# Decoder layer with a routed feed-forward on one Trainium2 core: six of the eight parts of the last batch's shared down product are made behind the last expert tile

## The reference, cut to what matters

```python
def relu2(x):
    r = jax.nn.relu(x)
    return r * r
...
topk_indices, topk_weights = _router(x, router_weight, e_bias)   # 2 of 16 experts for each token
combine = jnp.zeros((T, N_EXPERTS), ...).at[jnp.arange(T)[:, None], topk_indices].add(topk_weights)
h1 = jnp.einsum('th,ehi->tei', x, w_up)                          # 512 -> 256 for each expert
a = relu2(h1) * combine[:, :, None]
routed = jnp.einsum('tei,eih->th', a, w_down)                    # 256 -> 512
shared = relu2(hidden_states @ shared_up) @ shared_down          # 512 -> 1024 -> 512, all tokens
return routed.reshape(orig_shape) + shared
...
x = x + _L0_ffn_ref(_layernorm(x, axis=-1), ...)
```

## Time and profile before

| what | value |
|---|---|
| median of 3 runs | 1238.64 us (1237.73 to 1240.28) |
| the profiled execution | 1238.74 us, of which the profile's span is 1236.9 us |
| PE busy | 1073.2 us of the span (87%) |
| last down product of `close` on PE (L1243 with `attn`) | 27.6 us |
| 47 expert tiles on PE | from 1001.15 to 1199.3 us of the span |
| loading back, adding and storing | from 1202.78 to the end |

### The profile page before, as it was taken

The page is one execution under the profiler, slowest core; times in us unless marked ns, Lnnn a source line. Parts: engine busy times, 40 slices in busy tenths (PEclk is TensorE's granted clock), DMA queues, the critical chain, the costliest instruction groups (busy, mean ns, idle before and its releaser), DMA issues. The chain is left out here.

```text
span 1236.9 us, 18614 instructions
## 1 busy us (share of the span) xinstructions
PE 1073.2 (87%) x6368; PEld 642.0 (52%) x6368; DVE 806.6 (65%) x1195; ACT 668.3 (54%) x1438; POOL 673.2 (54%) x587
## 2 busy tenths in 40 slices
PE   7999838888888888888888899999999989999970
PEld 3444325555555555555555444444444457676740
DVE  5477779999999999999999476631760013333327
ACT  3566768889888888898888424202010012223220
POOL 1033369999999999999999630202041124444430
PEclk9999959999999999999999999999999999999995
DMA  6210001101111111111331212103027314333219
GB/s 204 87 36 19 18 18 35 35 28 35 35 36 32 30 35 36 36 33 63 95 102 45 90 48 103 69 34 116 20 79 244 102 44 128 127 128 129 77 49 385
DMA packets 51820, 94.74 MB, mean 77 GB/s; under 512 B 9806, under 2 KB 17998, under 8 KB 51728
## 3 DMA queue, kind: packets, MB, share of 16 engines
q1 hardware_dynamic: 44208, 72.82, 17.9%
q0 software_dynamic: 7520, 20.72, 5.4%
HBM read 74.51 MB, written 20.84 MB: 77 GB/s over the span
## 5 line engine op out<-in xcount | busy, mean ns | idle before, releaser
L604 POOL TENSOR_TENSOR w_all<-w_all 128x512 f32<-128x512 f32 x256 | 321.1, 1275 | 0.6 <-POOLq L96 0.3
L778 DVE TENSOR_TENSOR_SCAN w_all<-da,w_all 128x512 f32<-128x512 f32 x256 | 298.0, 1206 | 0.0
L712 ACT ACTIVATE da<-w_all,a_flat 128x512 f32<-128x512 f32 x256 | 179.6, 702 | 9.0 <-PEq L96 7.7
L683 PE MATMUL yb<-ident,w_all 128*128 128x128 f32 x1024 | 161.6, 281 | 7.5 <-DVE acc L786 7.5
L633 PE MATMUL sc<-w_all,attn 32*128 32x384 f32 (+3 forms) x512 | 105.0, 486 | 45.5 <-ACT w_all L720 22.8
L720 ACT ACTIVATE w_all<-sc,neg_max 128x128 f32<-128x128 f32 (+3 forms) x256 | 134.1, 539 | 16.5 <-DVE neg_max L770 15.5
L659 PE MATMUL ob<-w_all,v 128*32 128x128 f32 x1280 | 94.7, 277 | 52.8 <-ACT w_all L729 52.8
L683 PEld LDWEIGHTS yb<-ident,w_all 128*128 128x128 f32 x1024 | 113.5, 141 | 37.0 <-issue 30.6
L770 DVE TENSOR_REDUCE neg_max<-sc 128x2 f32<-128x256 f32 (+3 forms) x128 | 104.2, 814 | 34.2 <-PE sc L636 34.2
L1166 POOL TENSOR_TENSOR w_all<-w_all 128x512 f32<-128x512 f32 x24 | 29.4, 1226 | 165.0 <-ACT w_all L1337 165.0
L729 ACT ACTIVATE w_all<-tb 128x256 f32<-128x256 f32 (+2 forms) x192 | 102.8, 535 | 29.7 <-PE tb L648 29.7
(11 more groups left out here) (199 smaller groups left out, 1630.6 us busy)
## 6 DMA issues: line engine op xcount, KB each, us to landing
w_all<-b_scratch SPq DMA_DIRECT2D x64, 256.0 KB, 3.3
w_all<-in_w_up SPq DMA_DIRECT2D x16, 512.0 KB, 6.0
w_all<-in_w_down SPq DMA_DIRECT2D x16, 512.0 KB, 6.8
w_all<-sorted_y SPq DMA_DIRECT2D x16, 512.0 KB, 10.3
attn<-in_x SPq DMA_DIRECT2D x4, 1024.0 KB, 6.8
w_all<-in_x SPq DMA_DIRECT2D x16, 256.0 KB, 4.1
norms<-attn SPq DMA_DIRECT2D x4, 1024.0 KB, 4.3
out_dram<-acc SPq DMA_DIRECT2D x16, 256.0 KB, 8.9
```

Of the source, the lines that this page charges most:

```text
L604: pool.tensor_tensor(dbu[:, k, :], keep["du"][i // N][:, k * T:(k + 1) * T], b_all[i % 2][:, :], ALU.mult).then_inc(pool_dbu.sem, pool_dbu ...
L683: last = pe.transpose(yb[which][:, k * P:(k + 1) * P], state[i % 2][:, k, t * P:(t + 1) * P], ident[:, :])
L712: act.activation(da[unit % 2][:, :], keep["dt"][i // N][:, k * T:(k + 1) * T], ACT.Exp, scale=keep["a_flat"][:, unit % (N * KD):unit % (N ...
L778: dve.tensor_tensor_scan(state[i % 2][:, k, :], da[unit % 2][:, :], dbu[:, k, :], 0.0, ALU.mult, ALU.add).then_inc(dve_scan.sem, dve_scan. ...
```

## The change

For the last batch, `down(3, t)` in `close` uses only hidden parts m = 0 and 1 (`EARLY = 2`); DVE adds this partial sum to `acc` as before. The six other parts of each row tile, 24 matmuls, stand at the end of PE's list in `tiles`, behind the last tile's down product, and go to the PSUM banks 0 to 3. DVE adds each of these banks to `acc` just before the two weighted rows of row tiles 12 to 15, four more instructions in all.

The operands must outlive `close`, so they have other homes. `s_down` for the last batch comes in eight DMAs of 256 KB instead of one of 2 MB and lies in parts of `attn[1]` to `attn[3]`. The hidden parts lie in `attn[0]`, `attn[3]` and, the last four, in a new tile `late` of 8 KB for each partition. Until the router is done, `late` holds the router's small tensors, which had places of their own before; ACT therefore waits for `s_routed` before `relu(3)`. In `tiles` the buffers `x_t`, `h` and `h_t` move from `attn[2]` and `attn[3]` to `attn[0]` and `attn[1]`. Two counters of waits (`s_settle`, `s_settle_pe`) are now shared by two blocks.

```diff
+EARLY = 2
+LATE = 4 * T
...
-        s_down = [place(4, 2, D), attn[:, 2:4, :].rearrange("p b (k c) -> p (b k) c", c=D)]
-        h_t = [place(9, 2, T), attn[:, 0:2, :].rearrange("p b (k c) -> p (b k) c", c=T)]
+        s_down = place(4, 2, D)
+        h_t = place(9, 2, T)
+        r["h_last"] = [attn[:, 0, m * T:(m + 1) * T] for m in range(EARLY)] \
+            + [attn[:, 3, (m + 2) * T:(m + 3) * T] for m in range(2)] + [r["late"][:, m * T:(m + 1) * T] for m in range(4)]
+        r["s_down_last"] = [attn[:, 1, m * D:(m + 1) * D] for m in range(EARLY)] \
+            + [attn[:, 2 + m // 4, m % 4 * D:(m % 4 + 1) * D] for m in range(FK - EARLY)]
...
-            for b in range(2, B):
+            for b in range(1, B):
                 sp.wait_ge(s_keep[b].sem, s_keep[b].upto(0))
             sp.wait_ge(pe_nt.sem, pe_nt.upto(4 * LAST + 3))
-            sp.dma_start(s_down[1], d["s_down"].rearrange("(k p) n -> p k n", p=P)).then_inc(s_down_in[1].sem, s_down_in[1].tick(0))
+            for m in eight:
+                sp.dma_start(weights(LAST, m), d["s_down"][m * P:(m + 1) * P, :]).then_inc(s_down_in[1].sem, s_down_in[1].tick(m))
...
             def down(b, t):
-                out, w, h = down_bank(b, t), s_down[b // LAST], h_t[b // LAST]
+                out, end = down_bank(b, t), FK if b < LAST else EARLY
...
-                for m in eight:
+                for m in range(end):
                     if t == 0:
                         pe.wait_ge(pool_sq.sem, pool_sq.upto(FK * b + m))
-                    last = pe.matmul(out[:, :], h[:, m, t * P:(t + 1) * P], w[:, m, :], start=(m == 0), stop=(m == FK - 1))
+                    last = pe.matmul(out[:, :], hidden(b, m)[:, t * P:(t + 1) * P], weights(b, m), start=(m == 0), stop=(m == end - 1))
...
-            for b in range(2):
+            for b in (0, LAST):
                 act.wait_ge(s_keep[b].sem, s_keep[b].upto(0))
+            act.wait_ge(r["s_routed"], 1)
             relu(3, 0, 8)
...
-    x_t = [keep["attn"][:, 2, (2 + s) * D:(3 + s) * D] for s in range(2)]
-    h = [keep["attn"][:, 3, s * FE:(s + 1) * FE] for s in range(2)]
-    h_t = [keep["attn"][:, 3, (2 + s) * FE:(3 + s) * FE] for s in range(2)]
+    x_t = [keep["attn"][:, 0, (2 + s) * D:(3 + s) * D] for s in range(2)]
+    h = [keep["attn"][:, 1, 2 * D + s * FE:2 * D + (s + 1) * FE] for s in range(2)]
+    h_t = [keep["attn"][:, 1, 3 * D + s * FE:3 * D + (s + 1) * FE] for s in range(2)]
...
+        act_x.wait(pe, LAST, "xT")
+        dve_m.wait(pe, LAST, "sq")
+        for t in range(NT):
+            for m in range(EARLY, FK_S):
+                last = pe.matmul(bank[t][:, :], r["h_last"][m][:, t * P:(t + 1) * P], r["s_down_last"][m], start=(m == EARLY), stop=(m == FK_S - 1))
+            last.then_inc(s_late_out.sem, s_late_out.tick(t))
...
+            if t // NT == B - 1:
+                dve.wait_ge(s_late_out.sem, s_late_out.upto(t % NT))
+                dve.tensor_tensor(acc, bank[t % NT][:, :], acc, ALU.add).then_inc(s_late_add.sem, s_late_add.tick(t % NT))
+                dve.wait_ge(s_late_add.sem, s_late_add.upto(t % NT))
             for k in range(2):
```

More of the change, by code:

```diff
@@ L158, in project @@
         s_k, s_b, s_b_all = signal("k", 16), signal("b", 16), keep["s_b_all"]
-        s_const, s_settle, s_settle_pe = signal("const"), signal("settle"), signal("settle_pe")
+        s_const, s_settle, s_settle_pe = signal("const"), keep["s_settle"], keep["s_settle_pe"]
         pe_in, pe_xt, pe_q, pe_kv, pe_rows, pe_v, pe_c, pe_du, pe_dt = [
@@ L818, in __init__ @@
         TT = B * NT
+        taken = [0]
         def sb(name, shape, dt=F32):
-            return ctx.enter_context(nc.sbuf_tensor(name, shape, dt))
+            size = math.prod(shape[1:])
+            words = size if dt == F32 else size // 2
+            flat = r["late"][:, taken[0]:taken[0] + words]
+            taken[0] += words
+            assert taken[0] <= LATE
+            flat = flat if dt == F32 else flat.bitcast(dt)
+            if len(shape) == 3:
+                return flat.rearrange("p (a b) -> p a b", b=shape[2])
+            return flat
         self.bias = sb("bias", [P, E])
@@ L1072, in close, with hidden, weights @@
         s_up = place(2, 2, FS)
-        s_down = [place(4, 2, D), attn[:, 2:4, :].rearrange("p b (k c) -> p (b k) c", c=D)]
-        h_t = [place(9, 2, T), attn[:, 0:2, :].rearrange("p b (k c) -> p (b k) c", c=T)]
+        s_down = place(4, 2, D)
[4 more added lines that the diff above has]
+            + [attn[:, 2 + m // 4, m % 4 * D:(m % 4 + 1) * D] for m in range(FK - EARLY)]
+        def hidden(b, m):
+            return h_t[:, m, :] if b < LAST else r["h_last"][m]
+        def weights(b, m):
+            return s_down[:, m, :] if b < LAST else r["s_down_last"][m]
         x1 = keep["x1"]
@@ L1095, in close @@
         s_w_r, s_down_in = signal("w_r", 16), [signal(f"s_down{s}", 16) for s in range(2)]
-        s_eps, s_zero, s_settle_dve, s_settle_pe = [signal(n) for n in ("eps", "zero", "settle_dve", "settle_pe")]
+        r["s_late"] = s_down_in[1]
+        s_eps, s_zero, s_settle_dve, s_settle_pe = signal("eps"), signal("zero"), keep["s_settle"], keep["s_settle_pe"]
         pe_wo, pe_zt, pe_nt, pe_lg, pe_lt, pe_up, pe_down = [signal("pe_" + n) for n in ("wo", "zT", "nT", "lg", "lT", "up", "down")]
@@ L1123, in _ @@
             sp.dma_start(s_up[:, :, :], d["s_up"].rearrange("(k p) n -> p k n", p=P)).then_inc(s_up_in.sem, s_up_in.tick(0))
-            sp.dma_start(s_down[0], d["s_down"].rearrange("(k p) n -> p k n", p=P)).then_inc(s_down_in[0].sem, s_down_in[0].tick(0))
+            sp.dma_start(s_down, d["s_down"].rearrange("(k p) n -> p k n", p=P)).then_inc(s_down_in[0].sem, s_down_in[0].tick(0))
             save(0)
@@ L1162, in square @@
             def square(b):
-                h = h_t[b // LAST]
                 for m in eight:
                     pool.wait_ge(act_relu.sem, act_relu.upto(FK * b + m))
-                    pool.tensor_tensor(h[:, m, :], h[:, m, :], h[:, m, :], ALU.mult).then_inc(pool_sq.sem, pool_sq.tick(FK * b + m))
+                    pool.tensor_tensor(hidden(b, m), hidden(b, m), hidden(b, m), ALU.mult).then_inc(pool_sq.sem, pool_sq.tick(FK * b + m))
             for b in range(LAST):
@@ L1304, in _ @@
             up(3, 0, 8)
-            pe.wait_ge(s_down_in[1].sem, s_down_in[1].upto(0))
+            pe.wait_ge(s_down_in[1].sem, s_down_in[1].upto(FK - 1))
             for t in four:
@@ L1336, in relu @@
                         act.wait_ge(pe_down.sem, pe_down.upto(4 * b - 1))
-                    act.activation(h_t[b // LAST][:, m, :], bank[m % 2][:, :], ACT.Relu).then_inc(act_relu.sem, act_relu.tick(FK * b + m))
+                    act.activation(hidden(b, m), bank[m % 2][:, :], ACT.Relu).then_inc(act_relu.sem, act_relu.tick(FK * b + m))
             first_deviation(0)
@@ L1499, in experts @@
             "x_first": sb("x_first", [P, 2, D]),
+            "late": sb("late", [P, LATE]),
             "s_x": [ctx.enter_context(nc.semaphore(f"e_x{s}")) for s in range(4)],
@@ L1535, in tiles @@
     pair = Track(nc, ctx, "e_pair", ["first", "second"], 2)
+    s_late_out, s_late_add = keep["s_late_out"], keep["s_late_add"]
+    FK_S = FS // P
     LAST = SLOT_TILES - 1
@@ L1691, in decoder_layer @@
         keep["s_x"] = [Signal(nc, ctx, f"x_again{b}", 16) for b in range(B)]
+        keep["s_settle"], keep["s_settle_pe"] = Signal(nc, ctx, "settle"), Signal(nc, ctx, "settle_pe")
+        keep["s_late_out"], keep["s_late_add"] = Signal(nc, ctx, "late_out"), Signal(nc, ctx, "late_add")
         with ExitStack() as scan:
```

## The result

Median 1225.26 us over four runs (1223.83 to 1226.24), beside 1239.24 us for the kernel before on the same chips (four runs, 1237.73 to 1240.28). The ratio is 0.9888, with a 95% interval of 0.9874 to 0.9902: 14.0 us faster where 18.3 were forecast, and 1225.26 lies outside the range that ended at 1224.2. Over three comparisons the changed kernel has 13 runs with a median of 1225.24, while before had medians of 1239.24, 1240.38 and 1239.99 beside it. The gain between the medians was 14.0, 15.6 and 13.7 us, 14.5 in the mean.

The account below looks back on a forecast made before the run. PE bounds the kernel up to and through the expert tiles, then a chain of DVE additions in the last 30 us. Span 1236.9 - 18.6 + 0.3 = 1218.6, then + 1.84 - 0.1 = 1220.3 us median; range 1217.8 to 1224.2.

Parts of the forecast that it names:

- What is late next: the weights: Start of expert tiles: last weight DMA lands at 983.07, so first up product starts 18.6 us earlier, not 20.7.
- The clock at that gap: PE's idle gap before the first up product: low clock already paid before and after, no difference taken.
- a rival with 0.06: First expert tiles: the clock stays low for a further tile, up to 1224.4 us; chance 0.06.
- What is added at the end: Closing stretch: late PE matmuls end before DVE needs them; DVE gets 2.9 us more, the end moves 0.3 us.
- a store queue running dry: Last stores: 0.3 us for a queue dry for a moment, bounds 0 and DVE's full 2.9 us.
- DVE's part: Closing loop: four additions of 0.73 us each, 2.9 us; last addition ends at 1233.1 instead of 1230.16.
- The base: Starting time: span 1236.9 us; the profiled execution took 1.84 us more than its span, 0.10 more than the median.
- the first up product at 987.21 instead of 986 at the latest: Sign at the start of expert tiles: prediction wrong if the first up product starts later than 986; forecast near 983.9.
- the last store: Sign at the kernel's end: wrong if it lands 2 us or more behind its issue turn, near 1221; forecast 1218.0.
- "at four a us": Down product at 976 to 977: records go on at four a us, so DMA writes at 383 GB/s cost PE nothing.
- The steps costed at nothing: Before the tiles: eight `s_down` issues, waits for saved rows, ACT's router wait; in the tile loop, moved buffers: 0.
- the rival that forecast slower: Tile loop: new homes of `x_t`, `h`, `h_t` conflict with gathers; 1243.8 us at 0.5 us per tile; chance 0.05.

Follow-up runs that it names:

- homes only: Changed kernel with all eight parts of the last down product ahead of the expert tiles, no late matmuls or additions; 1239.41 us against 1240.38 for before, ratio 0.9996.
- four parts ahead: Changed kernel with four of eight parts of the last down product ahead of the expert tiles instead of two; 1225.52 us against 1240.77 for before, ratio 0.9878.

## Why the prediction was wrong

The mechanism and its place were right: the down product left the path, PE's late matmuls ended ahead of their additions, and the last weights became what the tiles start behind. Terms of the sum and the base were off. Means over the profiles, three with all eight parts ahead (before twice, homes only), three of the changed kernel:

- **What is late next: the weights.** Forecast 12.1 us from the start of the down product to the first up product, measured 12.8 to 13.0. The last DMA took 8.80 to 8.95 us in place of 8.5; the gathers, for which I had taken 0 and kept 0.6, were issued beside it, but no run isolates them. Its landing cost 1.11 to 1.21 us to the first matmul instead of 0.85: the reading of the number took what I took for it, but the matmul came 0.4 us behind it and not 0.05. The gain was 17.8 us, not 18.6: 0.8 lost.
- **The clock at that gap.** "The same cost is already in both. I take no difference" was the step that failed most. Of eight profiles in which PE was idle as long as before the change (about 2.5 us around one turn), three had one slow up product, five none; the profile I read was one of the three, so the cost was in fewer executions of before than I thought. Of the five profiles with the longer gap (5.2 to 5.4 us around the turn) and nothing in it, all had a slow first product and three a slow second. From the first up product to the last scatter it was 197.7 us in the mean of before and 199.5 after: 1.8 lost. The clock accounts for it: 197.2 us in all five profiles with the higher clock at both first products and nothing put into the gap, 197.7 to 198.7 where the shorter gap lost it, 198.2 to 201.0 where the longer one did. I had named this as a rival with 0.06. The Trainium skill (TensorE: Matmul & The Clock Gate, part 1) says both, that idleness brings the lower clock and that the point varies between runs; I read one execution as if it did not vary.
- **What is added at the end.** 0.3 us forecast for a store queue running dry, measured 1.0 from the first load on (34.1 to 35.1). DVE's part held: its last addition ends 3.4 us later behind the first load than before (1220.20 - 1189.41 against 1230.16 - 1202.78), but the last store, which took 6.2 us to land behind others, now lands 3.6 us behind its issue. Where the code load lies outside the closing stretch, the late work went with 0.3 us, as forecast. Left out of the sum was the code load of 16 KB, 0.95 us long, that fell among the loads in all three profiles of the changed kernel.
- **The base.** The profile and the median of before stood at 1238.6 to 1238.7, while before had 1239.24, 1240.38 and 1239.99 beside the changed kernel, 1.2 us more in the mean. The prediction took one median of three runs as exact.

0.8 + 1.8 + 1.0 - 0.3 is 3.3 us of lost gain: 15.0 us between the profiles from the start of the down product on, where 18.3 were forecast. The medians gained 14.5. The half us between, and the place of the 1.5 us by which `close` starts later in the three profiles of the changed kernel, stay open. In the first comparison, by itself, the gain was 4.3 us short and the base 0.6 us high. Of the signs that the prediction had named for being wrong, the first up product at 987.21 instead of 986 at the latest is none by itself, since `close` started 2.55 us later than in the profile of before; the last store, issued at 1220.4 and landed at 1224.0, is one even with 2.55 us taken off: 1221.4, where 1218.0 was forecast. One reading in the prediction was loose: down-product records do not go on "at four a us". Four records touch that us; one starts each 0.43 us. The argument from it stands, since the us from 982 with less traffic has the same row.

The steps costed at nothing (homes, eight issues, ACT's wait) cost nothing that was seen, and the tile's pace of 4.10 us was unchanged, so the rival that forecast slower is ruled out. The range was too narrow since each term was given its value from one profile.

What stays open: whether moving the code load alone would bring the last 1 us back; how much of the start of `close` belongs to the change; and why four parts ahead cost less in the median than PE's work.

## What to carry to other kernels

When work leaves the path, ask at once which transfer the next stage starts behind, and move its release too: here splitting the layout so that a third of the last weights could start earlier was worth another 5 us. Part of that is the clock, which this profile kept behind a gap of 2.5 us and three of eight such gaps lost. Price an idle gap of PE at the clock as well as at its length, and from more than one profile, since the same gap cost nothing in some executions and a slow stretch in others. Ask also where an engine's code is loaded: moved or added instructions move that load too, and beside full DMA engines it may not be free. A reader of one profile should take its distances between two instructions as measurements, but its distance to the median of later runs as unknown by a per mille or two.

## What the runs showed of the hardware

The clock's fall behind a short idle stretch is not a property of the program: the kernel before showed its first up product at 3.68 us in one profile and 1.99 in another. Four unused matmuls in the gap kept the clock at 2.4 GHz where five of five profiles without them lost it. One code load of 16 KB took 0.95 us of a DMA engine in the closing stretch, where the engines were full and the stretch 1.2 us longer in the mean; right behind the last scatter it took 1.16 to 1.44 us and put the first load 1.7 to 2.1 us later, in three profiles of three.
